# A decoder block on one core: one group of four rows, a denser mix of steps, two output areas, and two norms and the probabilities' scaling on ScalarE

## The reference

```python
x = layernorm(x + mamba2(x))                    # two layers of a selective scan, 512 channels, 64 states
x = layernorm(x + attention(ctx, ctx, x))       # one head, softmax over 256 keys
x = layernorm(x + moe(x))                       # 8 experts, hidden 1024, top 2 of them per token
# one layer of the scan, for each state s:  h = h * exp(dt * A[s]) + (dt * u) * B[s];  y += h * C[s]
# moe: out = sum over the two chosen experts e of weight_e * (w2_e @ relu(w1_e @ x + b1_e) + b2_e)
```

## Time and profile before

| what | us |
|---|---|
| median of 3 executions | 3298.54 |
| lowest, highest | 3296.21, 3299.12 |
| the profiled execution | 3306.1 |
| its span, first to last instruction | 3303.9 |
| DVE busy | 2989.0 (90%) |
| PE busy | 2864.8 (87%) |
| POOL busy | 2656.7 (80%) |
| ACT busy | 2649.0 (80%) |

### The profile page before, as it was taken

One profiled execution on the slowest core, in us unless ns is written; L12 is line 12 of the kernel. 1 busy time (PEld: TensorE's weight loads), 2 busy tenths in 40 slices (PEclk: granted clock), 3 DMA queues, 4 the chain that ended last, 5 costly groups with the idle time before them and its releaser, 6 DMA issues.

```text
span 3303.9 us, 58893 instructions
## 1 busy us (share of the span) xinstructions
PE 2864.8 (87%) x21429; PEld 2595.6 (79%) x21429; DVE 2989.0 (90%) x2141; ACT 2649.0 (80%) x6150; POOL 2656.7 (80%) x1289
## 2 busy tenths in 40 slices
PE   6889898988988799999868899989878879999676
PEld 5888888887877689888766788888767778899566
DVE  6999999999989999999999999999999999999610
ACT  6878888887978799898968689897977879988322
POOL 4889999888978898888988789797888878877501
PEclk8999999999999999999989899999989999999788
DMA  3342222222222335334221243524221143454176
GB/s 109 99 157 87 66 64 78 65 64 69 69 58 62 90 126 166 113 105 141 89 72 48 78 147 119 162 91 148 71 70 52 56 127 119 153 159 136 53 252 214
DMA packets 264660, 347.51 MB, mean 105 GB/s; under 512 B 88218, under 2 KB 157603, under 8 KB 263988
## 3 DMA queue, kind: packets, MB, share of 16 engines
q1 hardware_dynamic: 260418, 332.98, 32.5%
q0 software_dynamic: 3072, 8.39, 0.7%
q10 hardware_dynamic: 882, 2.38, 0.2%
HBM read 313.03 MB, written 30.62 MB: 104 GB/s over the span
## 4 chain that ended last, share of the span: by engine, by line
PE 33%; ACT 21%; DVE 17%; issue 14%; POOL 13%; DMA 2%; SPq 1%; DVEq 0%; POOLq 0%; ACTq 0%
POOL hC L1065 11%; ACT dA L1260 10%; DVE h L1292 9%; PE psY L1606 9%; PE psG L1545 8%; PE psX L1587 4%; DVE psX L1282 4%; PE psG L1632 4%; ACT xs L1231 3%; PE psX L1577 3%; PE psX L1545 2%; ACT gT L1114 1%; ACT hid L1215 1%; PE psX L1569 1%; DMA w_up<-in_w_exp 1%
## 5 line engine op out<-in xcount | busy, mean ns | idle before, releaser
L1065 POOL TENSOR_TENSOR hC<-h,cb 128x1024 f32<-128x1024 f32 x1024 | 2402.0, 2368 | 436.3 <-DVE h L1292 426.1
L1292 DVE TENSOR_TENSOR_SCAN h<-dA,psX 128x1024 f32<-128x1024 f32 (+1 forms) x1115 | 2303.7, 2101 | 83.4 <-ACT dA L1260 20.9
L1260 ACT ACTIVATE dA<-dt,negA 128x255 f32<-128x255 f32 x4096 | 1729.8, 510 | 180.1 <-DVE h L1292 178.4
L1606 PE MATMUL psY<-ident,hC 128*128 128x128 f32 x8192 | 1102.6, 279 | 47.9 <-DVE gT L1307 35.1
L1606 PEld LDWEIGHTS psY<-ident,hC 128*128 128x128 f32 x8192 | 956.3, 144 | 64.3 <-DVE gT L1307 38.2
L1282 DVE TENSOR_TENSOR psX<-dtu,psX 128x1024 f32<-128x1024 f32 x443 | 535.7, 1209 | 19.1 <-PE psX L1569 18.0
L1577 PE MATMUL psX<-ident,xs 128*128 128x128 f32 x2992 | 409.9, 282 | 115.2 <-ACT xs L1231 62.1
L1231 ACT ACTIVATE xs<-dtuT,bT 128x512 f32<-128x512 f32 x748 | 500.0, 723 | 1.3 <-PE psX L1577 1.2
L1577 PEld LDWEIGHTS psX<-ident,xs 128*128 128x128 f32 x2992 | 346.6, 145 | 169.4 <-ACT xs L1231 81.9
L1587 PE MATMUL psX<-diag_b,dtuT 128*128 128x128 f32 x3312 | 423.3, 282 | 39.2 <-DVE h L1292 37.4
L1587 PEld LDWEIGHTS psX<-diag_b,dtuT 128*128 128x128 f32 x3312 | 402.6, 197 | 68.5 <-issue 64.9
(11 more groups left out here) (213 smaller groups left out, 2056.7 us busy)
## 6 DMA issues: line engine op xcount, KB each, us to landing
cb<-c_dram SPq DMA_DIRECT2D x256, 512.0 KB
w_up<-in_w_exp SPq DMA_DIRECT2D x201, 256.0 KB, 3.1
...
diag_b<-b_dram SPq DMA_DIRECT2D x207, 128.0 KB, 3.6
...
```

What stands on the lines that cost most here:

```text
L1065: eng.tensor_tensor(hC[i % NHC][:, :, :], h[i % NH][:, :, :], cw.to_broadcast([P, KI, L]), ALU.mult).then_inc(times_c, 1)
L1260: made = eng.activation(dA[j % NA][:, c, 1:L], dt[n % 2][:, c, 1:L], ACT.Exp, scale=negA[:, JOBS[n][0], c, s:s + 1])
L1292: made = eng.tensor_tensor_scan(h[i % NH][:, part, :].rearrange("p c t -> p (c t)"), dA[i % NA][:, part, :].rearrange("p c t -> p (c t)"), ...
L1606: made = eng.matmul(psY[:, tc, c * P:(c + 1) * P], hC[i % NHC][:, c, tc * P:(tc + 1) * P], ident[:, :], start=s == 0 and c == 0, stop=s == ...
```

## The change

- **Groups.** Rows 0 to 3 form one group with 2*1024/128 + 7 = 23 tiles; [4, 5] and [6, 7] stay with 15 each. SLOTS doubles, from 4096 to 8192.
- **Kinds.** Jobs 1 to 9 have the mix of 22 P, 21 T, 21 M that jobs 1 to 5 had. Jobs 10 to 15 have 26 P, 25 T, 13 M; jobs 6 to 15 had 30 P, 25 T, 9 M.
- **Two output areas.** y_slots becomes a pair, taken in turn by groups. A group's first tile waits for the fetches of the group before the last, and so only where there is one. The clears become 4 areas x 16 = 64 transfers.
- **ScalarE.** norm1, norm2 and prob_norm go from DVE to ACT, as scale and bias of an ACTIVATE. The bias needs -mean * rstd, so `rstd` on POOL becomes three instructions for these two norms, with a wait between. ACT multiplies the maxima by -1/16 itself, and DVE keeps the maxima and the reciprocals. norm3 stays.
- **Tail.** The output tasks of rows 4 and 5 that stand in the tail are moved behind the 6th tile of the last group.
- The planner's costs of these tasks are changed to go with it.

```diff
--- before.py
+++ after.py
@@ -50,9 +50,9 @@
 PLAIN, ROWS_SCALED, BY_MATRIX = "PTM"
...
 EARLY = "PMT" * 21 + "P"
-LATE = "PTPMPTPTPMTPTPT" * 4 + "PTPM"
+LATE = "PTMPT" * 12 + "PTMP"
 FIRST_JOB = "P" * 13 + "TP" * 5 + "T" + EARLY[MATRIX_FROM:]
-KINDS = FIRST_JOB + EARLY * 5 + LATE * (NJ - 6)
+KINDS = FIRST_JOB + EARLY * 9 + LATE * (NJ - 10)
 KINDS = KINDS[:-1] + PLAIN
@@ -85,7 +85,7 @@
-GROUPS = [[0, 1], [2, 3], [4, 5], [6, 7]]
+GROUPS = [[0, 1, 2, 3], [4, 5], [6, 7]]
 GROUP_OF = {b: g for g, rows in enumerate(GROUPS) for b in rows}
@@ -119,7 +119,8 @@
 MARGIN = {"PE": 300, "ACT": 300, "POOL": -600}
...
 DUE = 4
-VECTOR_WORK = {"resid1", "norm1", "max", "prob_norm", "resid2", "norm2", "logit_max", "logit_sum", "top", "weights", "place", "list",
+OUTPUTS = {"acc_load", "fetch", "fetched", "blend", "bn3", "norm3", "stored"}
+VECTOR_WORK = {"resid1", "max", "prob_inv", "resid2", "logit_max", "logit_sum", "top", "weights", "place", "list",
                "b2_add", "blend", "bn3", "norm3"}
...
@@ -243,9 +244,10 @@
     then("q_copy", 0, "ACT", 2 * HALF_EVICT, frees=("q", b, 0))
...
     then("score+", 0, "PE", 2 * MM)
-    then("max", 0, "DVE", 900)
-    then("prob", 0, "ACT", 650, frees=("score", b, 0))
-    then("prob_norm", 0, "DVE", 1000)
+    then("max", 0, "DVE", 700)
+    then("prob", 0, "ACT", 850, frees=("score", b, 0))
+    then("prob_inv", 0, "DVE", 150)
+    then("prob_norm", 0, "ACT", 780)
     then("p_turn", 0, "PE", 4 * TURN, opens="G")
...
@@ -312,7 +314,7 @@
                                 opens="M" if half == i == 0 else None))
...
                 task("tile_out", t, 0, "DMA", 2500, ("y_copy", t, 0),
-                     *((("fetched", GROUPS[g - 1][-1], 0),) if g and t == TILE0[g] else ()))]
+                     *((("fetched", GROUPS[g - 2][-1], 0),) if g > 1 and t == TILE0[g] else ()))]
     for b in GROUPS[g]:
@@ -354,6 +356,11 @@
         self.bank_at.update(dict.fromkeys(("U0", "U1", "B0", "B1"), max(self.at.values())))
...
         self.span = max(self.at.values())
+
+        late = [x for x in self.tail if x[1] in GROUPS[-2] and (x[0] in OUTPUTS or x[0] == "rstd" and x[2] == 2)]
+        rest = [x for x in self.tail if x not in late]
+        at = rest.index(("out", TILE0[-2] + 5, (1, 3))) + 1
+        self.tail = rest[:at] + late + rest[at:]
@@ -690,11 +697,12 @@
         lists = [sb(f"lists{i}", [MAX_TILES, COMBOS]) for i in range(4)]
...
         x_slots = [nc.dram_tensor(f"x_slots{i}", [SLOTS, D], F32, kind="Internal").ap() for i in range(2)]
-        y_slots = nc.dram_tensor("y_slots", [SLOTS, D], F32, kind="Internal").ap()
+        y_slots = [nc.dram_tensor(f"y_slots{i}", [SLOTS, D], F32, kind="Internal").ap() for i in range(2)]
         kept = nc.dram_tensor("kept", [ROWS, P, KL, D], F32, kind="Internal").ap()
...
         rs = [small[:, at + 4:at + 6] for at in (0, 16, 40)]
+        shift = [small[:, at + 6:at + 8] for at in (0, 16)]
         mx, nm, rsum, rinv = (small[:, 8 + 2 * i:10 + 2 * i] for i in range(4))
...
@@ -749,7 +759,7 @@
                 eng.dma_start(source(0, b)[:, :, :], io["xT"][b]).then_inc(xT_in, 16)
...
             def clear(at):
-                tensor, part = (*x_slots, y_slots)[at // (CLEARS // 3)], at % (CLEARS // 3)
+                tensor, part = (*x_slots, *y_slots)[at // (CLEARS // 4)], at % (CLEARS // 4)
                 n = P * KL * 2
@@ -819,10 +829,10 @@
                 g = group_of_tile(t)
...
                 on.wait_ge(free[k], at + 1)
-                for b in GROUPS[g - 1] if g else ():
+                for b in GROUPS[g - 2] if g > 1 else ():
                     on.wait_ge(fetched[b], 16 * 4)
                 on.wait_ge(cleared, 16 * CLEARS)
-                eng.dma_start(y_slots[bass.DynSlice(tile_combo(t) * P, P), :], yg[:, :]).then_inc(y_tile_out, 16)
+                eng.dma_start(y_slots[g % 2][bass.DynSlice(tile_combo(t) * P, P), :], yg[:, :]).then_inc(y_tile_out, 16)
@@ -1024,11 +1034,17 @@
                             on.wait_ge(summed, STEPS)
...
                             on.wait_ge(blended, KL * n)
-                        eng.indirect_dma_start(got_of[n][:, tc, k, :], None, y_slots, bass.IndirectOffsetOnAxis(slot_of[:, n, k, tc:tc + 1], 0),
+                        eng.indirect_dma_start(got_of[n][:, tc, k, :], None, y_slots[GROUP_OF[n] % 2], bass.IndirectOffsetOnAxis(slot_of[:, n, k, tc:tc + 1], 0),
                                                bounds_check=SLOTS - 1, oob_is_err=False).then_inc(fetched[n], 16)
...
                         on.wait_ge(var_done[part], n + 1)
-                        eng.tensor_tensor(rs[part], mv[part][:, :, 1], neg_half[:, :], ALU.pow).then_inc(rstd_done[part], 1)
+                        if part == 2:
+                            eng.tensor_tensor(rs[2], mv[2][:, :, 1], neg_half[:, :], ALU.pow).then_inc(rstd_done[2], 1)
+                            continue
+                        eng.tensor_scalar(mv[part][:, :, 0], mv[part][:, :, 0], -1.0, None, ALU.mult).then_inc(power_done[part], 1)
+                        eng.tensor_tensor(rs[part], mv[part][:, :, 1], neg_half[:, :], ALU.pow).then_inc(power_done[part], 1)
+                        on.wait_ge(power_done[part], 2 * (n + 1))
+                        eng.tensor_tensor(shift[part], mv[part][:, :, 0], rs[part], ALU.mult).then_inc(rstd_done[part], 1)
@@ -1086,6 +1102,12 @@
                 else:
...
                     eng.activation(dst[:, 1, :], bank[k][:, L:2 * L], ACT.Identity, bias=bias[:, 1:2]).then_inc(free[k], 1)
+
+            def normalize(b, src, dst, i):
+                on.wait_ge(rstd_done[i], b + 1)
+                for tc in range(KL):
+                    made = eng.activation(dst[:, tc, :], src[:, tc, :], ACT.Identity, scale=rs[i][:, tc:tc + 1], bias=shift[i][:, tc:tc + 1])
+                made.then_inc(normed[i], 1)
@@ -1179,10 +1201,22 @@
                         k, at = turn["score", n, 0]
...
                         on.wait_ge(max_done, n + 1)
+                        own.mark(eng.activation(nm, mx, ACT.Copy, scale=-scale))
+                        on.wait_ge(s_own, own.value)
                         for tc in range(KL):
...
                         made.then_inc(free[k], 1)
+                    elif name == "prob_norm":
+                        on.wait_ge(inverted, n + 1)
+                        for tc in range(KL):
+                            made = eng.activation(prob[:, tc, :], prob[:, tc, :], ACT.Copy, scale=rinv[:, tc:tc + 1])
+                        made.then_inc(prob_done, 1)
+                    elif name == "norm1":
+                        normalize(n, xrow, x1, 0)
+                    elif name == "norm2":
+                        on.wait_ge(spilled, 16 * n)
+                        normalize(n, xrow, x2, 1)
                     elif name == "p_copy":
@@ -1392,29 +1426,18 @@
                         on.wait_ge(xrow_in, 16 * (n + 1))
...
                         moments(xrow, 0)
-                    elif name == "norm1":
-                        normalize(n, xrow, x1, 0)
                     elif name == "max":
...
                         on.wait_ge(full[k], at + 1)
-                        own.mark(eng.tensor_reduce(mx, two(k), AX_X, ALU.max))
-                        on.wait_ge(v_own, own.value)
-                        eng.tensor_scalar(nm, mx, -float(D) ** -0.5, None, ALU.mult).then_inc(max_done, 1)
-                    elif name == "prob_norm":
+                        eng.tensor_reduce(mx, two(k), AX_X, ALU.max).then_inc(max_done, 1)
+                    elif name == "prob_inv":
                         k, at = turn["score", n, 0]
                         on.wait_ge(free[k], at + 1)
-                        own.mark(eng.reciprocal(rinv, rsum))
-                        on.wait_ge(v_own, own.value)
-                        for tc in range(KL):
-                            made = eng.tensor_scalar(prob[:, tc, :], prob[:, tc, :], rinv[:, tc:tc + 1], None, ALU.mult)
-                        made.then_inc(prob_done, 1)
+                        eng.reciprocal(rinv, rsum).then_inc(inverted, 1)
                     elif name == "resid2":
...
                         moments(xrow, 1)
-                    elif name == "norm2":
-                        on.wait_ge(spilled, 16 * n)
-                        normalize(n, xrow, x2, 1)
                     elif name == "logit_max":
```

14 lines of the change are left out of this document (8 added, 6 removed).

## The result

The changed kernel took 3380.58 us (median of 4 runs, 3376.18 to 3388.07) beside 3298.83 us of the kernel before (3296.21 to 3302.07): ratio 1.025, 95% interval 1.0234 to 1.0266. It is 82 us slower where 64 us less were forecast. The profiled execution took 3376.9 us with a span of 3375.2, against 3303.9 before.

The account below looks back on a forecast made before the run. The prediction took DVE to bound the loop and PE time to price work pushed into the tail. Loop -98 us and tail +34 us made -64 us, from 3298.5 to 3234.5 us, range 3203 less 15 us up to 3272 us.

Parts of the forecast that it names:

- the tail's term: After the last scan: extra tiles +31 us, row 7's two norms 3 us, outputs of rows 4 and 5 0: +34 us.
- What bounds the kernel: Loop: DVE bounds it, 96% busy; steps taken off DVE are gained in full, work pushed into the tail costs PE time.
- Plain steps, 71 us: Loop: 57 fewer plain steps at 1.25 us each take 71 us off DVE.
- The loop's -98 us: Loop: -71 plain steps, -38 ScalarE, +3 matrix-step waits, +6 scaled-step waits, +2 clears give -98 us.
- Work moved to ScalarE, 38 us: Loop: norms, scalings, small multiplies and scan cuts leave DVE, 38 us gained; ScalarE and POOL were taken to have room.
- PE lateness, +3 us (0 to 10): Jobs 10 to 15: scans wait for PE at 24 more matrix steps among tiles, 3 us (0 to 10).
- the case in which PE bounds: Rival, 0.11: PE bounds jobs 10 to 15, 24 plain steps give nothing, 3264 us; sign: over 12 us DVE idle each.
- Groups: three tiles too few in the tail: Tiles per late job fall to 5.4 and 4.4, so 11 (bounds 4 and 15) are left for the tail.
- The WINDOW step: Planner sees 24 tasks of a chain, so no next-group tile is seen until two rows' outputs are placed.
- The rival on the slower side: Tiles fall out of the loop into the tail; point at 20 tiles left, 3322 us at 23; chance 0.04.
- The rival in which tiles keep their rate: Late jobs keep their tile rate, 4 tiles are left, tail +3 us, 3203 us; chance 0.20.
- The rival that ScalarE's part brings nothing: ScalarE becomes the bound, cannot follow in jobs with attention, the 38 us are lost, 3272 us; chance 0.06.

Follow-up runs that it names:

- run 4: Kernel before with the norms and scaling on ScalarE alone, plus the second output area and its clears: 3299.7 us, ratio 1.0000.
- run 6: Kernel before with all of the change's kinds and nothing else, groups of two, 57 plain steps fewer: 3330.0 us, ratio 1.0094.
- run 7: Kernel before with the group of four, two output areas and their clears, nothing else: 3313.8 us, ratio 1.005.
- run 5: Kernel before with the dense mix in jobs 6 to 9 too, 32 plain steps fewer, nothing else: 3272.0 us, ratio 0.9911.
- run 9: Kernel before with DVE's work kept, plus ScalarE's seven instructions a row into an unused buffer and POOL's three for one: 3332.8 us, ratio 1.0097.
- run 15: Kernel before in the task order planned when the added ScalarE and POOL instructions are counted, but none of them emitted: 3322.9 us, ratio 1.0073.
- run 3: Changed kernel with the old mix of kinds in jobs 10 to 15: 3297.0 us, ratio 0.9993 against the kernel before.
- Run 11: Changed kernel with the planner's WINDOW at 48 tasks instead of 24: 3317.6 us, ratio 1.0054 against the kernel before.
- Run 1: Changed kernel without moving the output tasks of rows 4 and 5 in the tail: 3373.5 us, ratio 1.0226 against the kernel before.
- run 2: Changed kernel with no expert tile tasks planned beside the last steps, from step 1023 on: 3370.7 us, ratio 1.0217 against the kernel before.
- run 16: Changed kernel with the old late mix, WINDOW 48, no tail reordering and no tiles beside the last step: 3272.05 us, ratio 0.9915.
- run 10: Kernel before with norm1, norm2 and the scaling cut to 16 of 256 columns on DVE: 3302.6 us, ratio 1.0004.

## Why the prediction was wrong

The loop gave 61 us of the 98, and the tail took 133 where 34 were forecast: the tail's term alone is off by 99 us. By the ratios of runs 4, 6 and 7 the parts alone are 0 + 31 + 17 = +48 us. Together they are +82, so some 34 us (give or take 10, by the intervals) come from the parts meeting, the reordering of the tail (7 us) among them. Step by step:

**What bounds the kernel: right, and followed too far.** The loop is DVE's, but that holds only while the tiles find room beside it. The second half of that sentence in the forecast, "what is pushed out of the loop into the tail is paid in PE time there", is most of the result.

**Plain steps, 71 us: the count right, the price too high.** 57 fewer came. Alone, the 32 early ones gave 0.9 us each (run 5, 0.7 to 1.2) and not 1.25, and the 25 late ones gave the loop nothing with groups of two (run 6). The loop's -98 us looked right up to the start of job 15 (-94) for a reason the forecast did not have: the outputs of rows 0 to 3, in jobs 8, 9, 12 and 13 before, had moved into job 15 and the tail. DVE's small work in jobs 8 and 9 together fell from 31.6 to 15.9 us, in job 15 it rose from 15.5 to 26.4.

**Work moved to ScalarE, 38 us: wrong.** DVE was relieved of 36 us (run 4), and the gain was 6 us in the loop, which is within what two executions differ by, and none in the time. The step that failed is "POOL is busy 162 of 187 us [...] so in the loop I take nothing", with "so that fits beside" for ScalarE: both counted room in busy shares and took the order of tasks as it was. What the same load costs with DVE unchanged is 33 us (run 9), and about 24 of these come with the order of tasks alone (run 15). That run 4's zero is the sum of these two is an inference, since its plan is not that of run 9. The price of one instruction was off too, but by little: a norm on ACT took 594 ns, not "at most 0.48 us"; on DVE it had taken 724 on the mean and 410 at the median. The rule of the Trainium skill, "ScalarE: Activation LUTs", section "Rules for kernel authors", to keep add and mul on VectorE, agrees with the outcome: no time was gained. No run shows that the price of the instructions is the reason.

**PE lateness, +3 us (0 to 10): too small.** DVE was idle 12.5, 15.4 and 13.4 us in jobs 11, 12 and 13, for 7.7, 7.1 and 7.6. That is 19 us in three jobs for a term of 3, and in three of the six late jobs, with job 15 in four, the forecast's own sign of the case in which PE bounds. Run 6, with groups of two, shows the same more strongly: 72 us idle in jobs 10 to 15 for run 5's 37.

**Groups: three tiles too few in the tail.** "I take 7 and 6. [...] 1.6 tiles. That leaves 5.4 and 4.4 a job." Measured: 4, 3, 5, 4. With the old mix the same group had 6, 5, 7, 5 (run 3), so the start was one too high in three of the four jobs, and the loss by four matrix steps was 2, 2, 2 and 1 tiles, near the 1.6. The estimate by PE's busy time missed that PE was not filled: job 10 has PE busy 165 of 182 us after, for 175 of 187 before, with three tiles fewer. The planner holds tiles back when its own costs say that the next step would be late. So group 0 was out 50 us into job 15, not 80 us into job 14. The WINDOW step, "no tile of the next group is seen until two rows' outputs are placed", was right: from then on one tile came in the loop. Run 11 prices it at 63 us. The sum was 14 tiles more in the tail for 11, near the end of the forecast's bounds (15). By the forecast's own arithmetic that is 23 + 7.25 x 15 = 132 us to the end of the first tile of the last group, +53 for +31: the count explains 22 of the 99 us.

**Tail, +34 us: +133, the step that cost most.** "Extra tiles fill that first" was the step that failed. The idle PE time of row 7's chain (38 us at the low clock, 23 at the full one) was counted as free for tiles. In this program's fixed order the tiles did not fill in around the chain; five stood in front of it. Row 7's last sums waited 32 us, and these tiles ran at 13 to 15 us each, waiting for their weights. Behind them, from 3096 to 3138 us, the chain has no tile evicted and PE busy 27 of 43 us, much as before (48 of 79). Then the tiles came every 7.25 to 8.1 us, with the 26 us hole by the outputs of rows 4 and 5, which were costed "0 us". So the 133 us are roughly 101 for 14 tiles at their full price, 19 for the hole beyond one tile's time, and 13 for all else. Run 1 and run 2 show that neither the hole nor the wait is worth more than some 10 us when taken away alone, since the tiles are still there. What a tile in the tail costs can be read roughly from 11: 59 us for 6. The forecast had 31 us for 11.

**The rival on the slower side had the mechanism** ("the tiles fall out of the loop"), but set its point at 20 tiles left and its price on top of a loop of -98. At 14 it came already, with a loop of -61. The rival in which tiles keep their rate (0.20) is what run 16 approaches, at 3272 us for its 3203, but it buys that with the old late mix: by the forecast's prices 31 of the missing 69 us are the 25 plain steps that it does not take away, and 38 the ScalarE term. The rival that ScalarE's part brings nothing was right in that part, at a chance of 0.06.

**The chances** were the worst part. The bounds of the tile count (4 to 15) were taken into the range by 29 us only, and the tail's price was linear in them with 7.25 us a tile and free room. Every mechanism that turned the sign stood in the forecast at a small size.

**What stays open:** how the some 34 us of meeting parts divide between group, mix and window; whether relieving DVE alone would be gained, which run 10 did not test; and what in run 15's order costs its 24 us (its jobs 6, 12 and 14 are longer, its job 11 shorter).
